# A state-space scan over two batch rows in one instruction, with the state set anew at the joint

## The reference

```python
def _ssm_scan(dA, dBx, C):
    def step(h, inp):
        dA_t, dBx_t, C_t = inp
        h = dA_t * h + dBx_t
        y = jnp.einsum('bdn,bn->bd', h, C_t)
        return (h, y)
    h0 = jnp.zeros(dA.shape[:1] + dA.shape[2:], dA.dtype)
    ...
delta = jax.nn.softplus(xc @ xd_w @ dtp_w + dtp_b)
Bm = xc @ xB_w
Cm = xc @ xC_w
A = -jnp.exp(A_log)
dA = jnp.exp(delta[..., None] * A)
dBx = (delta * xc)[..., None] * Bm[:, :, None, :]
y = _ssm_scan(dA, dBx, Cm) + D * xc
return y * jax.nn.silu(z) @ out_w + res
```

## Time and profile before

| | |
|---|---|
| median of 3 runs | 10,948.39 us (10,931.25 to 10,955.98) |
| profiled execution | 10,940.63 us |
| its span | 10,938.9 us, 153,072 instructions |
| busy DVE, PE, POOL, ACT (share of the span) | 8862.5 (81%), 8561.2 (78%), 7543.3 (69%), 5867.7 (54%) us |
| scans, all forms | 8192 instructions, 737 ns for most |
| POOL's products B times u | 4096, mean 1234 ns |
| DMA | 730.20 MB, mean 67 GB/s |

### The profile page before, as it was taken

How to read it: one execution, slowest core, us unless ns; L and a number is a source line. 1 busy time by engine, 2 the same in 40 slices (tenths; PEclk the granted TensorE clock), 3 DMA queues, 4 the chain that set the end, 5 groups by cost and what they waited for, 6 DMA issues and landing times. The chain is left out here.

```text
span 10938.9 us, 153072 instructions
## 1 busy us (share of the span) xinstructions
PE 8561.2 (78%) x42776; PEld 6924.1 (63%) x42776; DVE 8862.5 (81%) x13553; ACT 5867.7 (54%) x8819; POOL 7543.3 (69%) x7270
## 2 busy tenths in 40 slices
PE   6777777777777777777777777777777776899998
PEld 5666666666656566666566666566666665677776
DVE  5999989998999898989898999999999996233332
ACT  4555555555555555555555555555555553444443
POOL 5888888888888888888888888888888885000000
PEclk8888888888888888888888888888888887999999
DMA  2212222222222221222222222221222221000000
GB/s 84 84 65 70 74 84 78 84 78 78 79 76 82 78 79 58 77 78 84 78 84 78 84 74 83 77 76 59 79 78 84 78 76 53 8 12 12 10 10 10
DMA packets 366114, 730.20 MB, mean 67 GB/s; under 512 B 143670, under 2 KB 188890, under 8 KB 365274
## 3 DMA queue, kind: packets, MB, share of 16 engines
q1 hardware_dynamic: 361560, 717.54, 18.6%
q10 hardware_dynamic: 3714, 2.89, 0.1%
HBM read 699.27 MB, written 21.05 MB: 66 GB/s over the span
## 5 line engine op out<-in xcount | busy, mean ns | idle before, releaser
L488 POOL TENSOR_TENSOR bu<-b_all,u_buf 128x514 f32<-128x514 f32 x4096 | 4956.7, 1234 | 117.5 <-DVE h_ps L904 62.2
L713 ACT ACTIVATE decay<-delta,neg_a 128x512 f32<-128x512 f32 x3712 | 2546.0, 689 | 2976.1 <-DVE h_ps L904 2067.9
L904 DVE TENSOR_TENSOR_SCAN h_ps<-decay,bu 128x256 f32<-128x256 f32 x5534 | 3761.7, 737 | 410.3 <-ACT decay L713 243.3
L1151 PE MATMUL y_ps<-ident,ch 128*128 128x128 f32 x16384 | 2667.8, 311 | 907.9 <-DVE ch L920 440.5
L1151 PEld LDWEIGHTS y_ps<-ident,ch 128*128 128x128 f32 x16384 | 2202.8, 161 | 1405.9 <-DVE ch L920 651.0
L497 POOL TENSOR_TENSOR ch<-ch,c_all 128x512 f32<-128x512 f32 x1024 | 1429.5, 1396 | 1372.3 <-DVE ch L904 1372.2
L920 DVE TENSOR_TENSOR ch<-h_ps,c_all 128x512 f32<-128x512 f32 x3072 | 1977.3, 671 | 0.0
L904 DVE TENSOR_TENSOR_SCAN ch<-decay,bu 128x256 f32<-128x256 f32 x1890 | 1388.2, 735 | 1.0
L1036 PE MATMUL w_ps<-xn,in_w 128*128 128x257 f32 x4096 | 1087.8, 411 | 166.1 <-ACT xn L604 102.9
L1036 PEld LDWEIGHTS w_ps<-xn,in_w 128*128 128x128 f32 x4096 | 801.7, 208 | 328.3 <-issue 100.4
L1494 POOL TENSOR_TENSOR rstd_F<-h_F 128x514 f32<-128x514 f32 x16 | 17.5, 1095 | 1434.4 <-DMA h_F<-h_mid 1434.4
(11 more groups left out here) (250 smaller groups left out, 11649.4 us busy)
## 6 DMA issues: line engine op xcount, KB each, us to landing
b_all<-bc_dram SPq DMA_DIRECT2D x512, 514.0 KB, 8.2
c_all<-bc_dram SPq DMA_DIRECT2D x512, 514.0 KB, 9.4
in_w<-in_L_attn_in_w SPq DMA_DIRECT2D x64, 1024.0 KB, 5.0
x_in<-in_x SPq DMA_DIRECT2D x128, 256.0 KB, 2.6
out_w<-in_L_attn_out_w SPq DMA_DIRECT2D x64, 512.0 KB, 3.9
h_mid<-h_cur SPq DMA_DIRECT2D x32, 257.0 KB, 2.1
h_F<-h_mid SPq DMA_DIRECT2D x16, 514.0 KB, 3.7
out<-o_sb SPq DMA_DIRECT2D x64, 86.0 KB
```

Source lines behind the costliest of these rows:

```text
L488: pool.tensor_tensor(bu[:, s % NBU, :, :].rearrange("p b s -> p (b s)"), b_all[:, n // NU, n % NU, :, :].rearrange("p b s -> p (b s)"), u_ ...
L713: func(decay_slot(jj, s).rearrange("p (b t) -> p b t", b=NB), delta[:, c, :, 1:S], ACT.Exp, scale=neg_a[:, k, c, n:n + 1]).then_inc(decays ...
L904: last = dve.tensor_tensor_scan(h[:, cols], decay_slot(jj, s)[:, cols], bu[:, s % NBU, b, 1:], bu[:, s % NBU, b, 0:1], ALU.mult, ALU.add)
L1151: last = pe.matmul(y_ps[:, k, :], ch[:, s % NPR, k * P:(k + 1) * P], ident[:, :], is_transpose=True, start=False, stop=(n == NST - 1 and k ...
```

## The change

The last token of row 0 and the second of row 1 become neighbours, and for 48 of the 64 states (channel groups 1 to 3) one scan of 512 runs over both.

- **Layout.** A state's 514 numbers in `b_all`, `c_all`, `u_buf` and `bu` are now: the first token of both rows, then 256 of row 0, then 256 of row 1. Position `JOINT` = 258 is token 1 of row 1. `bring_bc` stores to `bc_dram` with two DMAs instead of one; the loads back are the same.
- **The joint.** `delta` at that token is set to 1e20 once and left out of every later write (`JOINT_SIDES`: two additions instead of one), so that the decay there is exp(-large) = 0. `neg_a` is kept below -1e-17. `u_buf` there is 1, and `b_all` there holds the full value of h at token 1, gain * u0 * B0 + u1 * B1, so that the product gives it.
- **What makes that value**, on DVE for channel groups 1 to 3: `joint_step` (delta of tokens 0 and 1 of row 1), `joint_u` (times x), `joint_carried` (gain * u0 * B0 for 16 states), `set_joint` (adds u1 * B1, writes 8 states of `b_all`, twice per group). `keep_rows` once per job copies the B values that the joint overwrites, and waits for all eight pairs of loads. On ACT `joint_gain` (an exponential over 16 numbers) in units 3, 6 and 7. POOL waits for `joints_set` ahead of the first product of each half group.
- **Channel group 0** is scanned row by row as before.
- **Slots.** The two PSUM slots for h alternate over the states that use them (`h_slot`), no more by the parity of s.
- **NDS** is 2 instead of 3.

```diff
-NBU, NPR, NDP, NDS = 4, 8, 2, 3
+JOINT = NB + L
+NBU, NPR, NDP, NDS = 4, 8, 2, 2
+JOINT_SIDES = slice(0, S + 1), slice(S + 2, 2 * S)
+RESET = 1e20
+LEAST_A = 1e-17
...
-                sp.dma_start(rows, dtbc[RNK:, :, :].rearrange("r b s -> r (b s)")).then_inc(bc_stored, 16)
+                sp.dma_start(rows[:, 0:NB], dtbc[RNK:, :, 0], allow_slow_non_contiguous=True).then_inc(bc_stored, 16)
+                sp.dma_start(rows[:, NB:].rearrange("r (b t) -> r b t", b=NB), dtbc[RNK:, :, 1:]).then_inc(bc_stored, 16)
...
+            pool.memset(delta[:, 1:, 1, 1:2], RESET).then_inc(zeros_set, 1)
+            pool.memset(u_buf[:, 1, JOINT:JOINT + 1], 1.0).then_inc(zeros_set, 1)
...
-                pool.tensor_tensor(delta[:, c, :, :], sp_l[c % 2], sp_r[c % 2], ALU.add).then_inc(delta_ready, 1)
+                if c == 0:
+                    pool.tensor_tensor(delta[:, c, :, :], sp_l[c % 2], sp_r[c % 2], ALU.add).then_inc(delta_ready, 1)
+                else:
+                    for cols in JOINT_SIDES:
+                        last = pool.tensor_tensor(flat(delta[:, c, :, :])[:, cols], flat(sp_l[c % 2])[:, cols],
+                                                  flat(sp_r[c % 2])[:, cols], ALU.add)
+                    last.then_inc(delta_ready, 1)
 
             def delta_x(g, jj, c):
                 pool.wait_ge(delta_ready, job_count(g, jj, CI, c + 1))
                 if c == 0:
                     pool.wait_ge(xc_ready, job_count(g, jj, 1, 1))
-                pool.tensor_tensor(u_buf[:, c % 2, :, :], delta[:, c, :, :], xc[:, jj % 2, c, :, :], ALU.mult).then_inc(u_ready, 1)
+                u, x = u_buf[:, c % 2, :], xc[:, jj % 2, c, :, :]
+                pool.tensor_tensor(u[:, 0:NB], delta[:, c, :, 0], x[:, :, 0], ALU.mult)
+                if c == 0:
+                    last = pool.tensor_tensor(u[:, NB:].rearrange("p (b t) -> p b t", b=NB), delta[:, c, :, 1:], x[:, :, 1:], ALU.mult)
+                else:
+                    if c == 2:
+                        pool.memset(u[:, JOINT:JOINT + 1], 1.0)
+                    pool.tensor_tensor(u[:, NB:JOINT], delta[:, c, 0, 1:], x[:, 0, 1:], ALU.mult)
+                    last = pool.tensor_tensor(u[:, JOINT + 1:], delta[:, c, 1, 2:], x[:, 1, 2:], ALU.mult)
+                last.then_inc(u_ready, 1)
...
+                if c > 0 and n % PAIRS == 0:
+                    pool.wait_ge(joints_set, job_count(g, jj, 2 * (CI - 1), 2 * (c - 1) + n // PAIRS + 1))
...
-                h = ch[:, s % NPR, :].rearrange("p (b t) -> p b t", b=NB)
-                pool.tensor_tensor(h, h, c_all[:, n // NU, n % NU, :, 1:], ALU.mult).then_inc(pool_c_done, 1)
+                h = ch[:, s % NPR, :]
+                pool.tensor_tensor(h, h, c_all[:, n // NU, n % NU, NB:], ALU.mult).then_inc(pool_c_done, 1)
...
+                    if c == 3:
+                        act.wait_ge(step_01_ready, job_count(g, jj, CI - 1, c - 2))
...
+            def joint_gain(g, jj, c):
+                k = BLOCK_OF_JOB[jj % 4]
+                act.wait_ge(step_01_ready, job_count(g, jj, CI - 1, c))
+                func(gain_1[:, c, :], neg_a[:, k, c, :], ACT.Exp, scale=step_01[:, c, 1:2]).then_inc(gain_1_ready, 1)
...
+                if u in (3, 6, 7):
+                    joint_gain(g, jj, {3: 1, 6: 2, 7: 3}[u])
...
+            def h_slot(s):
+                return len([v for v in range(s) if v not in POOL_C]) % NU
+            def keep_rows(g, jj):
+                for n in range(PAIRS):
+                    dve.wait_ge(bc_loaded[n], job_count(g, jj, 32, 32))
+                dve.tensor_copy(b_keep[:, :, :], b_all[:, :, :, 1:JOINT + 1:JOINT - 1].rearrange("p n i t -> p t (n i)")
+                                ).then_inc(b_kept, 1)
+            def joint_step(g, jj, c):
+                dve.wait_ge(sp_sums, job_count(g, jj, 2 * CI, 2 * c + 2))
+                dve.tensor_tensor(step_01[:, c, :], sp_l[c % 2][:, 1, 0:2], sp_r[c % 2][:, 1, 0:2], ALU.add
+                                  ).then_inc(step_01_ready, 1)
+            def joint_u(g, jj, c):
+                dve.wait_ge(step_01_ready, job_count(g, jj, CI - 1, c))
+                if c == 1:
+                    dve.wait_ge(xc_ready, job_count(g, jj, 1, 1))
+                dve.tensor_tensor(u_01[:, c, :], step_01[:, c, :], xc[:, jj % 2, c, 1, 0:2], ALU.mult).then_inc(u_01_ready, 1)
+            def joint_carried(g, jj, c):
+                if c == 1:
+                    dve.wait_ge(b_kept, job_count(g, jj, 1, 1))
+                dve.wait_ge(u_01_ready, job_count(g, jj, CI - 1, c))
+                dve.wait_ge(gain_1_ready, job_count(g, jj, CI - 1, c))
+                dve.scalar_tensor_tensor(out=carried[:, c, :], in0=gain_1[:, c, :], scalar=u_01[:, c, 0:1], in1=b_keep[:, 0, :],
+                                         op0=ALU.mult, op1=ALU.mult).then_inc(carried_ready, 1)
+            def set_joint(g, jj, c, half):
+                part = slice(half * PAIRS, (half + 1) * PAIRS)
+                dve.wait_ge(carried_ready, job_count(g, jj, CI - 1, c))
+                dve.wait_ge(b_done, job_count(g, jj, STATES, NST * (c - 1) + (half + 1) * PAIRS))
+                dve.scalar_tensor_tensor(out=b_all[:, :, :, JOINT].rearrange("p n i -> p (n i)")[:, part], in0=b_keep[:, 1, part],
+                                         scalar=u_01[:, c, 1:2], in1=carried[:, c, part], op0=ALU.mult, op1=ALU.add
+                                         ).then_inc(joints_set, 1)
             def scan(g, jj, s, b):
                 inside = s not in POOL_C
                 if b == 0:
                     dve.wait_ge(decays_ready, job_count(g, jj, STATES, s + 1))
                     dve.wait_ge(b_done, job_count(g, jj, STATES, s + 1))
-                    if inside and positive(c_count(g, jj, s - NU)):
-                        dve.wait_ge(c_done, c_count(g, jj, s - NU))
+                    if inside and positive(c_count(g, jj, s) - NU):
+                        dve.wait_ge(c_done, c_count(g, jj, s) - NU)
                     if not inside and positive(job_count(g, jj, STATES, s + 1 - NPR)):
 
                         dve.wait_ge(y_added, job_count(g, jj, STATES, s + 1 - NPR))
-                h = h_ps[:, s % NU, :] if inside else ch[:, s % NPR, :]
+                h = h_ps[:, h_slot(s), :] if inside else ch[:, s % NPR, :]
+                if s >= NST:
+                    dve.tensor_tensor_scan(h, decay_slot(jj, s), bu[:, s % NBU, NB:], bu[:, s % NBU, 0:1],
+                                           ALU.mult, ALU.add).then_inc(scan_done, 1)
+                    return
                 cols = slice(b * L, (b + 1) * L)
-                last = dve.tensor_tensor_scan(h[:, cols], decay_slot(jj, s)[:, cols], bu[:, s % NBU, b, 1:],
-                                              bu[:, s % NBU, b, 0:1], ALU.mult, ALU.add)
+                last = dve.tensor_tensor_scan(h[:, cols], decay_slot(jj, s)[:, cols], bu[:, s % NBU, NB + b * L:NB + (b + 1) * L],
+                                              bu[:, s % NBU, b:b + 1], ALU.mult, ALU.add)
...
                     s = NU * u
                     scan(g, jj, s, 0)
-                    scan(g, jj, s, 1)
+                    if s < NST:
+                        scan(g, jj, s, 1)
+                    if u in (0, 3, 4):
+                        joint_step(g, jj, {0: 1, 3: 2, 4: 3}[u])
                     if size:
                         step_size(*size, 0)
                     scan(g, jj, s + 1, 0)
-                    if s + 1 in POOL_C:
-                        c_times_h(g, jj, s)
+                    if s < NST:
+                        if s + 1 in POOL_C:
+                            c_times_h(g, jj, s)
                         scan(g, jj, s + 1, 1)
-                    else:
-                        scan(g, jj, s + 1, 1)
+                    if u in (0, 3, 4):
+                        joint_u(g, jj, {0: 1, 3: 2, 4: 3}[u])
+                    if s + 1 not in POOL_C:
                         c_times_h(g, jj, s)
                         c_times_h(g, jj, s + 1)
+                    elif s >= NST:
+                        c_times_h(g, jj, s)
+                    if u == 3:
+                        keep_rows(g, jj)
+                    if u % PAIRS == 4 and u < 3 * PAIRS:
+                        joint_carried(g, jj, u // PAIRS + 1)
+                    if u % PAIRS == 5 and u < 3 * PAIRS:
+                        set_joint(g, jj, u // PAIRS + 1, 0)
+                    if u % PAIRS == 1 and u > PAIRS:
+                        set_joint(g, jj, u // PAIRS, 1)
```

54 lines of the change are left out of this document (33 added, 21 removed).

## The result

The kernel after takes 11,018.3 us in the median of four runs (11,009.5 to 11,032.4), the kernel before 10,943.0 beside it (10,931.3 to 10,956.0): a ratio of 1.007, 95% interval 1.0052 to 1.0087. That is +75 us, or 1.2 us in each of the 64 jobs; forecast were +48 us (10,996) and "slower" at 0.50. So the sign and the size came out. The runs show that the two largest terms behind it were both too large, and that two things stand in it which the prediction did not have at all; that they left a sum so near the forecast was luck.

A forecast was written before the change was run, and what follows sets the result against it. VectorE (DVE) was taken as busiest, 91% in the state-space phase. Terms -3.7 - 1.0 - 0.55 - 0.8 + 6.8 = +0.75 us per job, 64 jobs: +48 us, 10,996 us; range 10,790 to 11,140.

The forecast's parts named there:

- two early decays: Ahead of ACT's Silu blocks: the chain starts one decay sooner, -1.0; fewer dear early scans in job 3, -0.55 us per job.
- wide scans: DVE, 48 states per job: one 512 scan for two of 256 saves 0.11 us per state; 34 count, -3.7 us per job.
- small operations on DVE: Sixteen added instructions per job for the joint, many stalled behind POOL: +6.8 us per job.
- the waits for POOL that they cover: Units 0 to 5: new DVE work covers two waits for POOL's products, -0.8 us per job.
- that leaves 36, 24, 40 and 36 of 48: States in the four jobs whose scan saving counts, the rest lying ahead of DVE waits for TensorE and ACT; mean 34.
- Not much smaller: Sign: DVE's waits for output rows (257 us) and decays (243 us) stay near their totals though their chains start sooner.
- 0.52 each: Price in us of a small two-input DVE operation beside busy POOL, from L931's mean of 552 ns; bounds 0.1 and 1.1.
- The rival of starved operations: Some small operations wait behind several POOL products: mean price 0.8, +4.3 us per job, 11,220 us; chance 0.10.
- Nothing: POOL's waits on joints_set were forecast to cost nothing, since the write comes before POOL asks for it.
- Cheap: Rival: small DVE operations cost 0.3 us each, as POOL is mostly between instructions then: -2.0 us, 10,820 us; chance 0.30.
- The wide scan is faster: Rival: a 512 scan on DVE takes less than two cycles per element, 8.8 us more saved, 10,430 us; chance 0.05.
- Cancel: Rival: gains and costs cancel, with small DVE operations at 0.46 us each, 10,948 us; chance 0.15.

The follow-up runs named there:

- run 5: The kernel before with two early decays (NDS 2) in place of three, nothing else: 10,861.4 us, ratio 0.9920.
- run 9: The kernel after without small operations, all scans of 256 columns, h_ps slots by state number modulo 2 as before: 10,814.8 us, ratio 0.9880.
- run 8: The kernel after without the small operations and with each 512-column scan cut in two of 256: 10,772.3 us, ratio 0.9839.
- run 1: The kernel after without its sixteen small DVE operations per job, the three gains on ACT and their waits: 10,678.6 us, ratio 0.9762.
- run 3: The kernel after with each 512-column scan cut into two of 256, the joint kept: 11,112.3 us, ratio 1.0154.
- run 7: The kernel after with fifteen one-column DVE fills ahead of everything, moving the loop's start by fifteen places: 10,990.0 us, ratio 1.0042.
- run 10: The kernel after with the joint worked out on POOL and one early decay per Silu block in place of two: 10,774.6 us, ratio 0.9844.

## Why the prediction was right, step by step

The runs take the change apart in a chain: before, run 5 (two early decays), run 9 (the rest without slots), run 8 (slots), run 1 (wide scans), after (small operations). Per job is the difference over 64.

| step | forecast, us per job | measured | us in all |
|---|---|---|---|
| two early decays | -1.55 | -1.3 | -83 |
| slots of h_ps, layout, order | none | -1.4 | -47 - 43 |
| wide scans | -3.7 | -1.5 | -94 |
| small operations on DVE, less the waits for POOL that they cover | +6.8 - 0.8 | +5.3 | +340 |
| sum | +0.75 | +1.2 | +75 |

(The parts add to +73 us; the two that are missing are within the scatter of the medians. The sizes hold in this order: beside the small operations the wide scans gave 122 us, not 94.)

**The sum was luck.** The scans gave 2.2 us per job less than forecast and the decays 0.25 less; against that, the small operations cost 0.7 less, and 1.4 came from parts that the prediction had not priced. The direction was argued rightly, since the small operations do cost more than the wide scans save, but four errors that nearly cancel put the total within 27 us.

**The scans.** The duration was right, 1276 ns for 1.27 us. What was wrong is the step "that leaves 36, 24, 40 and 36 of 48": it took 34 states in 48 to count. DVE's busy time fell by 391 us, 6.1 per job, and 94 us came out, a quarter. The list of stretches that give a saving back had only units 12 to 18 and 25 to 27 and the four states ahead of the wait after unit 11. But a wait of 2 to 4 us that is there takes up what is saved between it and the one before it, and where that wait was zero a new one comes up: the waits for output rows and decays grew from 119 to 129 and from 75 to 116 in number, and by 234 us together. Beside the small operations more is left: run 3 has 271 us more busy time than run 7, and 122 more of time. "Not much smaller" the prediction said of the two waits; ahead of the small operations they grow, and the small operations then fill them again, which is why the page shows 257 and 243 before and 256 and 231 after.

**The small operations.** "0.52 each" was mis-sized: it is 0.82. It came from one row, the 552 ns of line 931, which runs once per job at one place. The rival of starved operations had the right mean (0.8) and the wrong time (11,220), because it counted 12.5 of 15 on the path. Of 12.5 us per job 5.3 reached the end: the 787 + 11 us gave 560 of busy time (160 went into other operations that then stand behind POOL), and 177 us of that fell into the three waits of run 1. The two errors, +0.3 on the price and the share that counts, went opposite ways. Included in the 340 are 28 to 41 us that have nothing to do with them, the gap at the loop's turn: it came with the number of instructions ahead of the loop, a step the prediction had not thought of.

**The decays** were near in size, with more of it in DVE's busy time than the prediction had, and run 10 shows where the saving turns round. **POOL** was right as it was argued, new DVE work that covers waits for POOL's products: 153 us without the small operations (run 1), 87 with them, 1.0 us per job for the forecast 0.8; it is inside the +5.3. What the table has at -1.4 is something else. The slots of h_ps, 43 us, and the layout and order, 47, were in the diff and had no term in the sum. "Nothing" for the waits on joints_set, for the copy of rows (173 ns each) and for ACT's exponentials stands: no row of the waits names them.

**The rivals.** "Cheap" fell with the 0.82 us. "The wide scan is faster" fell with 1276 ns. "Cancel" was 70 us off, outside the 0.2%.

## What to carry to other kernels

Before an operation is put on the vector engine beside a busy GpSimd, ask what it touches, not how long it is: with every tile in SBUF an operation on eight columns took 0.5 to 1 us here in the mean and 3 at worst (one on sixteen columns 6), with one input in PSUM 0.15, and on GpSimd itself some 0.2 to 0.3. A change whose large part saves and whose small part costs should be split before it is judged: here the change with its joint on GpSimd was worth 2.1%, of which the wide scans themselves are less than half (94 us of 240), and sixteen tiny instructions in the wrong queue turned it into a loss. Of time saved on an engine that waits for two others, count only what the waits behind it leave, which was between a quarter (94 of 391 us) and a half (122 of 271) here.
